# Unnormalised exponentials in the memory attention, an epsilon moved to GpSimd, and a folded column operation in a two-layer decoder

## The reference, cut to what matters

```
x = x + attention(ln(x))              # 16 heads of 128, softmax
x = x + linear_attention(ln(x), ctx)  # "lin", 16 heads of 16
x = x + nf4_ffn(ln(x))                # "ffn", 704 hidden
x = x + feature_attention(ln(x))      # "fat"
x = x + memory_attention(ln(x), ctx)  # "mem"
x = x + ternary_ffn(ln(x))            # "ter", 1024 hidden
```

```
# mem: 16 heads of 16, 64 memory tokens a batch
x = rmsnorm(hidden_states, norm_w)                     # eps 1e-6
attn = softmax(where(mask, q @ k.T * scale, -inf))     # over 64 tokens
out = (attn @ v) @ wo.T ; return sigmoid(x @ wg.T) * out
# ter: w1, w2 ternary with scales s1, s2
h = square(relu(x @ w1)); hmax = max(max(h), 1e-5)
h = round(h / hmax * 255) / 255 * hmax ; return h @ w2
```

## Time and profile before

| | us |
|---|---|
| median of 3 runs | 919.81 |
| lowest and highest | 917.97, 923.12 |
| the profiled execution, whole | 922.4 |
| its span | 920.4 |

### The profile page before, as it was taken

One profiled execution on the slowest core, in us unless ns is written; L12 is line 12 of the kernel. 1 busy time (PEld: TensorE's weight loads), 2 busy tenths in 40 slices (PEclk: granted clock), 3 DMA queues, 4 the chain that ended last, 5 costly groups with the idle time before them and its releaser, 6 DMA issues. The chain is left out here.

```text
span 920.4 us, 18709 instructions
## 1 busy us (share of the span) xinstructions
PE 853.7 (93%) x6868; PEld 634.0 (69%) x6868; DVE 720.4 (78%) x1759; ACT 535.1 (58%) x1277; POOL 368.4 (40%) x354
## 2 busy tenths in 40 slices
PE   4788988999999999999999998999988889999786
PEld 3455766777777777777777776887855578787554
DVE  5748878878888788778887775897698779876885
ACT  1435576655665666556655744555566864545576
POOL 4103456545554455455555554043233031521410
PEclk9989999999999999999999998999999999999999
DMA  9123231011101110111000000000000010000001
GB/s 280 36 71 69 54 96 35 2 35 35 34 0 34 34 34 6 28 34 34 18 16 11 1 1 1 1 2 1 1 2 1 1 47 1 1 1 1 2 1 46
DMA packets 34722, 25.56 MB, mean 28 GB/s; under 512 B 9492, under 2 KB 31596, under 8 KB 34668
## 3 DMA queue, kind: packets, MB, share of 16 engines
q1 hardware_dynamic: 34380, 24.56, 10.3%
q10 hardware_dynamic: 288, 0.26, 0.1%
HBM read 22.65 MB, written 2.17 MB: 27 GB/s over the span
## 5 line engine op out<-in xcount | busy, mean ns | idle before, releaser
L483 POOL CAST exp_hi<-exp_scores 128x1024 f16<-128x1024 f32 x64 | 67.0, 1047 | 212.9 <-ACT exp_scores L596 212.9
L485 POOL TENSOR_TENSOR exp_lo<-exp_scores,exp_hi 128x1024 f16<-128x1024 f32 x64 | 140.7, 2199 | 5.1
L596 ACT ACTIVATE exp_scores<-banks,exp_bias,unscale 128x256 f32<-128x256 f32 x256 | 141.0, 560 | 2.1
L75 PE MATMUL banks<-value_out_hi,xn_t_hi 128*128 128x256 f16 x512 | 139.6, 273 | 0.3 <-DVE X L931 0.3
L76 PE MATMUL banks<-value_out_lo,xn_t_hi 128*128 128x256 f16 x512 | 139.6, 273 | 0.0
L77 PE MATMUL banks<-value_out_hi,xn_t_lo 128*128 128x256 f16 x512 | 139.6, 273 | 0.0
L1124 PE MATMUL banks<-qk 128*128 128x256 f32 x512 | 121.6, 380 | 9.0 <-ACT exp_scores L596 8.9
L1124 PEld LDWEIGHTS banks<-qk 128*128 128x128 f32 x512 | 96.6, 190 | 30.3 <-issue 9.6
L931 DVE SCALAR_TENSOR_TENSOR X<-banks,colsum,X 128x256 f32<-128x256 f32 x256 | 106.2, 477 | 11.0 <-DVE colsum L922 9.6
L575 ACT ACTIVATE qk<-banks 128x512 f32<-128x512 f32 x128 | 75.8, 601 | 57.9 <-PE banks L77 57.9
L906 DVE TENSOR_REDUCE neg_rowmax<-banks 128x4 f32<-128x1024 f32 x64 | 78.2, 1221 | 27.9 <-PE banks L1124 27.9
(11 more groups left out here) (253 smaller groups left out, 1973.9 us busy)
## 6 DMA issues: line engine op xcount, KB each, us to landing
head_weights<-in_wqkv_d SPq DMA_DIRECT2D x32, 128.0 KB, 3.7
weight_absmax_rows<-across_partitions SPq DMA_DIRECT2D x15, 256.0 KB, 4.0
X<-in_x_d SPq DMA_DIRECT2D x4, 512.0 KB, 7.3
head_weights<-in_wqkvt_d SPq DMA_DIRECT2D x16, 128.0 KB, 3.5
head_weights<-in_w_o_d SPq DMA_DIRECT2D x16, 128.0 KB, 3.5
out<-X SPq DMA_DIRECT2D x8, 256.0 KB, 2.1
ternary_then_kv_and_rows<-in_c_fc_d SPq DMA_DIRECT2D x1, 1024.0 KB, 6.2
ternary_then_kv_and_rows<-in_c_proj_d SPq DMA_DIRECT2D x1, 1024.0 KB, 8.0
```

Source lines behind the costliest of these rows:

```text
L75: nc.tensor.matmul(out, lhs[0], rhs[0], start=first, stop=False)
L483: nc.gpsimd.tensor_copy(probh[:, s1_.par], prob[:, s1_.par]).then_inc(exph_ready, 1)
L485: nc.gpsimd.tensor_tensor(probl[:, s1_.par], prob[:, s1_.par], probh[:, s1_.par], ALU.subtract).then_inc(expl_ready, 1)
L596: last = nc.scalar.activation(prob[:, s1_.par, t, :], sc_ps[t // ST][:, t % ST, :], ACT.Exp, bias=nbias[:, t:t + 1], scale=unscale[:, s1_. ...
```

## The change

- **Memory attention.** `pn` is gone. `pt` waits for `exp` and transposes the exponentials as they are. `sum` and `rd` stay, but now beside `pt`, `pte`, `o` and `ote`. The reciprocals of the sums go to the other layout in three new stages: `rw` on ACT (two ACTIVATEs per tile, 128x128 each, which spread 8 reciprocals over 16 columns each into `xt_stream`, free by then), `spread` on PE (two fp32 matmuls per tile, `xt_stream` as weights and the identity as moving side, into the free half of `PA`), `on` on DVE (one multiply per tile of 128x256, `ot_stream` times that half bank). `mem_o` is now raised by `on`.
- **Norms.** `eps` moves from DVE to POOL, just ahead of `pow`, for all 36. `aggr` raises `mv`, on which POOL waits; `pow` still waits for `veps`, now raised by its own engine.
- **Ternary.** sqrt(255) is folded into a scale worked out once at the start (L981 makes `tscale_root` in place of `tscale255`), so that `c0`'s reciprocal is the scale that `sq` needs, and `c1` is gone.
- **The planner's list.** The new stages have lengths of their own (`rw` .45, `spread` .46, `on` .33, `eps` .2 on POOL), `aggr` goes from .16 to .24, and the order of all four engines is worked out anew.

The diff, cut to its core:

```diff
-    NORM = ["stats", "aggr", "eps", "sh", "xn", "lo"]
+    NORM = ["stats", "aggr", "sh", "xn", "lo"]
...
-        return [f"{layer}_stats DVE .66 {after}", f"{layer}_aggr DVE .16", f"{layer}_eps DVE .08", f"{layer}_pow POOL .67",
+        return [f"{layer}_stats DVE .66 {after}", f"{layer}_aggr DVE .24", f"{layer}_eps POOL .2", f"{layer}_pow POOL .67",
...
-                                         "pn POOL 1.86", "pt PE 1.02", "pte ACT .92", "o PE .58", "ote ACT .36")]
+                                         f"pt PE 1.02 mem{t}_exp", "pte ACT .92", "o PE .58", "ote ACT .36",
+                                         f"rw ACT .45 mem{t}_rd", "spread PE .46", f"on DVE .33 mem{t}_ote mem{t}_spread")]
...
-                                         f"relu ACT 1.0 ter{t}_max", f"c0 DVE .24 ter{t}_m0", "c1 DVE .08",
-                                         f"sq ACT 1.04 ter{t}_relu ter{t}_c1", "n DVE .6", "nt PE .45", "nte ACT .91",
+                                         f"relu ACT 1.0 ter{t}_max", f"c0 DVE .24 ter{t}_m0",
+                                         f"sq ACT 1.04 ter{t}_relu ter{t}_c0", "n DVE .6", "nt PE .45", "nte ACT .91",
...
+            if part == "eps":
+                ln = norms[layer]
+                pool.wait_ge(ln["mv"], nth_norm(layer, s))
+                inside, eps = (1.0 + 1e-6, LN_EPS * 1e-6) if layer == "mem" else (1.0, LN_EPS)
+                nc.gpsimd.tensor_scalar(rstd[s][:, :], mv[s][:, :, 1], inside, eps, ALU.mult, ALU.add).then_inc(ln["veps"], 1)
...
-            elif part == "pn":
-                t = tile_of(layer)
-                pool.wait_ge(mem_rden[t], n[s])
-                nc.gpsimd.tensor_tensor(by_head(s), by_head(s), den[s][:, t, :].unsqueeze(2).broadcast_to([P, XH, M]),
-                                        ALU.mult).then_inc(mem_pn[t], 1)
...
+            elif part == "rw":
+
+                t = tile_of(layer)
+                act.wait_ge(mem_rden[t], n[s])
+                inverse = den[s][:, t, :].rearrange("p (r k c) -> p k r c", k=KT, c=4)
+                for k in range(KT):
+                    last = nc.scalar.activation(
+                        xt[s][:, t, k * P:(k + 1) * P].rearrange("p (r c e) -> p r c e", c=4, e=XD),
+                        inverse[:, k].unsqueeze(3).broadcast_to([P, 2, 4, XD]), ACT.Copy)
+                last.then_inc(mem_rwide[t], 1)
...
+            elif part == "on":
+
+                dve.wait_ge(mem_oraw[t], n[s])
+                dve.wait_ge(mem_spread[t], n[s])
+                cols = ot[s][:, :, t * P:(t + 1) * P]
+                nc.vector.tensor_tensor(cols, cols, PA[s][:, KT * P:2 * KT * P].rearrange("p (k n) -> p k n", k=KT),
+                                        ALU.mult).then_inc(mem_o[t], 1)
...
-                pe.wait_ge(mem_pn[t], n[s])
+                pe.wait_ge(mem_exp[t], n[s])
...
+            elif part == "spread":
+
+                pe.wait_ge(mem_rwide[t], n[s])
+                for k in range(KT):
+                    last = nc.tensor.matmul(PA[s][:, (KT + k) * P:(KT + k + 1) * P], xt[s][:, t, k * P:(k + 1) * P],
+                                            g.ident[:, :], start=True, stop=True)
+                last.then_inc(mem_spread[t], 1)
```

More of the change, by code:

```diff
@@ L980, in step @@
                 nc.vector.reciprocal(trec[:, :], g.tscale[:, :]).then_inc(tern, 1)
-                nc.vector.tensor_scalar(g.tscale255[:, :], g.tscale[:, 1:2], 1.0 / 255.0, None, ALU.mult)
+                nc.vector.tensor_scalar(g.tscale_root[:, :], g.tscale[:, 0:1], float(255.0 ** -0.5), None, ALU.mult)
                 dve.wait_ge(mask_loaded, 16)
@@ L1264, in norm_sems @@
     def norm_sems(name):
-        return {k: sem(f"{name}_{k}") for k in ("veps", "rstd", "xn", "xt_full", "xt_ready", "added")}
+        return {k: sem(f"{name}_{k}") for k in ("mv", "veps", "rstd", "xn", "xt_full", "xt_ready", "added")}
     lin, ffn, fat, mem, ter = (norm_sems(k) for k in ("lin", "ffn", "fat", "mem", "ter"))
@@ L1287, in streams_part @@
     two = lambda k: [sem(f"mem_{k}{t}") for t in range(ST)]
-    mem_s_full, mem_max, mem_sub, mem_exp, mem_sum, mem_rden, mem_pn = (
-        two(k) for k in ("s_full", "max", "sub", "exp", "sum", "rden", "pn"))
-    mem_pt_full, mem_pt, mem_o_full, mem_o = (two(k) for k in ("pt_full", "pt", "o_full", "o"))
+    mem_s_full, mem_max, mem_sub, mem_exp, mem_sum, mem_rden, mem_spread = (
+        two(k) for k in ("s_full", "max", "sub", "exp", "sum", "rden", "spread"))
+    mem_pt_full, mem_pt, mem_o_full, mem_oraw, mem_o, mem_rwide = (
+        two(k) for k in ("pt_full", "pt", "o_full", "oraw", "o", "rwide"))
     mem_out, mem_go = (sem(f"mem_{k}") for k in ("out", "go"))
@@ L1368, in stage @@
         def stage(s, name, layer, part):
-            if part == "pow":
+            if part == "eps":
[3 more added lines that the diff above has]
+                nc.gpsimd.tensor_scalar(rstd[s][:, :], mv[s][:, :, 1], inside, eps, ALU.mult, ALU.add).then_inc(ln["veps"], 1)
+            elif part == "pow":
                 ln = norms[layer]
@@ L1514, in norm_stage @@
             elif part == "aggr":
-                dve.wait_ge(norm_step[s], s // STREAMS * 2 * len(norms) + 2 * nth - 1)
+                dve.wait_ge(norm_step[s], s // STREAMS * len(norms) + nth)
                 dve.sem_inc(turn, 1)
@@ L1518, in norm_stage @@
                     last = nc.vector.bn_aggr(mv[s][:, t, :], st6[s][:, t, :])
-                last.then_inc(norm_step[s], 1)
-            elif part == "eps":
-                dve.wait_ge(norm_step[s], s // STREAMS * 2 * len(norms) + 2 * nth)
-                if layer == "mem":
-                    nc.vector.tensor_scalar(rstd[s][:, :], mv[s][:, :, 1], 1.0 + 1e-6, LN_EPS * 1e-6, ALU.mult,
-                                            ALU.add).then_inc(ln["veps"], 1)
-                else:
-                    nc.vector.tensor_scalar(rstd[s][:, :], mv[s][:, :, 1], LN_EPS, None, ALU.add).then_inc(
-                        ln["veps"], 1)
+                last.then_inc(ln["mv"], 1)
             elif part == "sh":
@@ L1656, in ternary_stage @@
                 dve.wait_ge(ter_max[t], n[s])
-                nc.vector.tensor_scalar(small[s][:, 5:6], small[s][:, 4:5], g.tscale[:, 0:1], float(np.sqrt(1e-5)),
-                                        ALU.mult, ALU.max).then_inc(ter_step[s], 1)
+                nc.vector.tensor_scalar(small[s][:, 5:6], small[s][:, 4:5], g.tscale_root[:, 0:1],
+                                        float(np.sqrt(1e-5 / 255.0)), ALU.mult, ALU.max).then_inc(ter_step[s], 1)
             elif part == "c0":
-                dve.wait_ge(ter_step[s], s // STREAMS * 3 * ST + 3 * t + 1)
-                nc.vector.reciprocal(small[s][:, 6:7], small[s][:, 5:6]).then_inc(ter_step[s], 1)
+                dve.wait_ge(ter_step[s], s // STREAMS * 2 * ST + 2 * t + 1)
+                nc.vector.reciprocal(small[s][:, 7:8], small[s][:, 5:6]).then_inc(ter_scale[t], 1)
                 nc.vector.tensor_scalar(small[s][:, 9 + t:10 + t], small[s][:, 5:6], small[s][:, 5:6],
-                                        g.tscale255[:, 0:1], ALU.mult, ALU.mult).then_inc(ter_step[s], 1)
-            elif part == "c1":
-                dve.wait_ge(ter_step[s], s // STREAMS * 3 * ST + 3 * t + 2)
-                nc.vector.tensor_scalar(small[s][:, 7:8], small[s][:, 6:7], float(np.sqrt(255.0)), None,
-                                        ALU.mult).then_inc(ter_scale[t], 1)
+                                        g.tscale[:, 1:2], ALU.mult, ALU.mult).then_inc(ter_step[s], 1)
             elif part == "n":
@@ L1978, in decoder @@
     g.tscale = sb("ternary_scale", [P, 2])
[L1979 removed]
+    g.tscale_root = sb("ternary_scale_root", [P, 1])
     g.small_loads, g.early_loads = [], []
```

5 lines of the change are left out of this document (2 added, 3 removed).

## The result

The changed kernel takes **917.90 us** (median of 22 runs, 915.39 to 920.25); before, measured alongside, it takes 919.94 (917.97 to 923.12). The ratio is 0.9972, with a 95% interval of 0.9963 to 0.9982: 2.0 us less by the medians and 2.6 by the ratio, under 0.5% either way; the interval leaves no change out. Forecast was 916.8 us, 3.0 less.

The account below looks back on a forecast made before the run. PE bounds one stretch, DVE nearly the memory stage, tile hand-over between engines the ternary stage. Terms -1.0 - 1.4 - 0.8 + 0.8 - 0.6 = -3.0 us give 916.8 us; range 909.5 to 926, the forecast's own 913 to 921.

Parts of the forecast that it names:

- What bounds the kernel: Per stretch: PE fills 604 to 672 us, DVE nearly bounds the memory stage, no engine fills the ternary stage.
- Prices of the operations: New instructions: `on` 0.41 us, each `rw` ACTIVATE 0.3, `spread` 0.5 a tile, POOL's `eps` 0.2.
- Memory, the engines: Memory stage: DVE's 1.6 us and PE's 1.7 of remaining room limit the gain; 0.5 us a round, -1.0 in all.
- rival 2: Memory stage: the shorter chain's gain arrives in full, 3.6 us a round, 910.6 us; chance 0.27.
- Epsilon: Norms: hold-up and order at ternary norms -1.4 us, DVE steps in its bound stage -0.8, POOL's price and wait +0.8.
- rival 3: Norms: POOL's `eps` dear or held up, 0.4 us more each on eight norms, 919.2 us; chance 0.09.
- Ternary: Ternary stage: sixteen `c1` leave DVE and the squares wait less for it, -0.6 us, bounds 0 and -2.8.
- Clock: PE's idle gaps: the new order may spare a clock fall or bring one each round, +-1.7 us, taken as none.
- rival 1: Memory stage: `on` waits in DVE's in-order list for ACT and PE, 8 us lost in all, 925.8 us; chance 0.22.

Follow-up runs that it names:

- the epsilon's operation alone: Kernel before with epsilon issued by POOL just ahead of `pow`, planner's list and every engine's order unchanged: 920.75 us, ratio 1.0009.
- the epsilon part's own order: Order planned when only the epsilon's move to POOL, operation and list entry, is made to the kernel before: 928.46 us, ratio 1.0092.
- the ternary order alone: Kernel before with `c1` dropped from the planner's list but still issued right behind `c0`: 916.84 us, ratio 0.9962.

## Why the prediction held, point by point

The time was right within 1.1 us, the sum behind it much less so: its errors cancel, and that the total came so close is luck. The largest term of the forecast, the epsilon's, isn't there, and the largest that was measured, the clock's, was put at 0.

- **What bounds the kernel**: right. The stretches bound by PE took 73.21 us before and after in both rounds. But "every term here rests on the PE-bound stages staying as they are" was a condition on the order that I had no way to price: two orders break it.
- **Prices of the operations**: right, each within 10%.
- **Memory, the engines** (-1.0): the two stages shrank by 0.9 in all, as forecast, but not by this part, which alone gives +0.1; the epsilon's entry in the list moved them. By the marks the stage went from 32.95 to 32.48; the "32 us now" of the forecast was the window from 672 to 704. The limit was right in kind: DVE had 1.6 us of room. The step missed is that PE would reach the end of its room at the same time; I set it down (1.7 left) and used only the smaller.
- **The chain in full (rival 2)** didn't come true: 1.8 us less of chain a tile brought nothing (33.00 us with the memory part alone), while PE and DVE filled up to 31.4 and 32.1 of it. (The range's lower end, 909.5, should have been 908.9 by its own terms, 910.6 less 1.7.)
- **Epsilon** (-1.4 - 0.8 + 0.8): failed. The operation is worth nothing, and my two gains aren't there. The stall of 0.95 us was on the chain as printed, and I saw none in the second round; it is there too, at 874.25. Moved to POOL alone, it only turns into a wait for `pn`, so the 0.8 can't be had without the memory part; beside it, `pow` ends 1.06 us behind `aggr`, and the whole operation is worth the 0.4 above. The 0.5 us a round at stream 3's ternary norm did arrive there (in the epsilon's operation alone `pow` ends 1.06 us behind `aggr` for 2.13 before), but the join behind it takes 69.09 us for 68.96: nothing hung on it. The 0.8 for DVE's steps was 0.1 a round in the first stretch (73.13 for 73.21). The price was right: POOL's pair takes 1.06 us where nothing holds it up and DVE's and POOL's took 0.98, 0.08 more for the 0.1 I took. With the entry, by the sums of the table less 1.6 for each fall, the epsilon is worth +6 alone, -0.8 beside the memory part and +2 beside memory and ternary part.
- **POOL's epsilon held up (rival 3)**: seen once in the tail, with no price that shows. Timeline of the kernel after (start, length):

```profile
878.39 0.66 DVE L1629 SCALAR_TENSOR_TENSOR X<-gate_stream,X 128x512 f32<-128x512 f32 x1
878.56 0.54 POOL L1375 TENSOR_SCALAR rstd_stream<-mv_stream 128x2 f32<-128x2 f32 x1 [2.96 <-DVE mv_stream L1530]
```

  It takes 0.54 us for 0.205 and ends as DVE's addition, with two SBUF inputs, does. The Trainium skill ("SBUF — State Buffer", section "Who interferes with whom") states that a DVE instruction with two SBUF inputs contends with a GpSimd instruction that reads SBUF, and that what they share is an exclusive lock. The trace agrees: 878.56 + 0.54 is 879.10, and the addition ends at 879.05.
- **Ternary** (-0.6): the term for the operation was about right (0.12 us in each of the two stretches that hold it, so 0.2). The order of its entry is worth 2.6 more by itself, and I had put it at nothing. In the full change it isn't to be seen: memory plus epsilon, without it, has the same 315.9, and there PE's list is the same with the ternary entry or without.
- **Clock** (0, within 1.7): a fall was spared, which the text named as possible. It is the largest single term, 1.6 us by the marks (one fall) and about 1.6 by the table (2.3 us less lacking, at 0.7).
- **Waits ahead of `on` (rival 1)**: none (idle 0.0). With `spread` doubled, DVE waits 1.7 us for it in six places, so the mechanism exists from a price of about twice what it costs.

So the sum reads: work -1.1 by the stretches, clock about -1.6, together -2.7, against -2.0 by the medians and -2.6 by the ratio; the forecast had work -3.0, clock 0.

## What to carry to other kernels

Where lengths in a list set the order of all engines, a changed entry is an edit of its own, often larger than the operation it stands for (here -4 to +12 us against 0 to 0.4): measure the operation in the old order and the old operation in the new order, and keep the best pair. Before costing work moved off a chain, look at which engines fill the gap: when two are nearly full, the shorter chain brought nothing here, more work on one of them cost, and relieving one alone brought 0.1 us. Compare stretches between marks, not spans, and take out clock falls by comparing two executions of the same stage.

## What the hardware showed that I hadn't expected

- A fall of the granted clock to the 1.2 GHz level in a memory stage costs 1.58 us (34.54 for 32.96, twice in different kernels with the same figures). In the kernels that show it PE idles 5.7 us of the stage (8.6 in the epsilon part's own order); in the ternary order alone it idles the same 5.7, and the profiled execution has no fall there.
- Two fp32 transposes are two records where two fp32 matmuls are four (L1846, x64; L1844 with transposes, x32), and their weight loads take 0.14 us for 0.19. As a price that is 0.55 us a tile for about 0.27, at the same result; the memory stage kept its clock at 1.00.
